# A decoder layer on one core: attention numerator computed transposed, x transposed by DMA, and a new order on every engine

## The reference, cut to what matters

```python
# 1. linear attention with positive features phi (64 per head)
phi = (exp(proj(x) - |x|^2 / (2 sqrt(d))) + 1e-6) / sqrt(m)
kv, ksum = phi_k^T v, sum(phi_k)
out = (phi_q kv) / (phi_q . ksum);   x = layernorm(x + out @ Wo.T + bo)
# 2. softmax attention: queries from x, keys and values from ctx_1024
x = layernorm(x + softmax(q k^T / 4) v)
# 3. gated FFN, 256 -> 1024 -> 256: weights rounded to -1, 0, 1 (scale = mean |w|),
#    activations rounded to 8 bits (scale = row maximum)
x = layernorm(x + bitlinear(silu(bitlinear(x, w_gate)) * bitlinear(x, w_up), w_down))
```

## Time and profile before

| | |
|---|---|
| median of 3 runs | 566.46 us (565.43 to 566.99) |
| the profiled execution, its own time | 565.91 us |
| span of that execution (first to last instruction) | 564.2 us |
| PE busy | 486.1 us (86%) |
| DVE busy | 472.4 us (84%) |
| ACT busy | 411.2 us (73%) |
| POOL busy | 387.6 us (69%) |

### The profile page before, as it was taken

How to read it: one execution, slowest core, us unless ns; L and a number is a source line. 1 busy time by engine, 2 the same in 40 slices (tenths; PEclk the granted TensorE clock), 3 DMA queues, 4 the chain that set the end, 5 groups by cost and what they waited for, 6 DMA issues and landing times.

```text
span 564.2 us, 17426 instructions
## 1 busy us (share of the span) xinstructions
PE 486.1 (86%) x5932; PEld 345.5 (61%) x5990; DVE 472.4 (84%) x1380; ACT 411.2 (73%) x811; POOL 387.6 (69%) x768
## 2 busy tenths in 40 slices
PE   3056999999999998999999999999999998977651
PEld 2034766677667676777777777777777776654320
DVE  0784565889999998999999999999999998998671
ACT  0226667778888887888888888888888887867531
POOL 7032665677777777788777777788788876665432
PEclk9576999999999999999999999999999999998765
DMA  5604776566877775556565656566555587473111
GB/s 142 221 0 82 138 133 110 87 122 122 135 131 133 132 125 110 125 124 131 117 130 120 130 118 130 119 129 124 121 125 123 124 124 122 87 113 67 41 45 37
DMA packets 192649, 64.14 MB, mean 114 GB/s; under 512 B 172384, under 2 KB 192352, under 8 KB 192608
## 3 DMA queue, kind: packets, MB, share of 16 engines
q1 hardware_dynamic: 190080, 60.46, 55.3%
q10 hardware_dynamic: 2528, 3.15, 1.7%
HBM read 17.31 MB, written 4.19 MB: 38 GB/s over the span
## 4 chain that ended last, share of the span: by engine, by line
PE 60%; DVE 12%; DMA 9%; ACT 7%; issue 4%; SPq 4%; POOL 4%; ACTq 0%; POOLq 0%; DVEq 0%
PE bank L1084 9%; PE bank L1151 8%; PE bank L1274 5%; DMA hqT<-hq 5%; PE bank L1244 5%; PE bank L1297 4%; PE bank L1167 3%; PE bank L1104 3%; PE bank L1149 3%; PE bank L1133 2%; PE bank L1099 2%; PE bank L1181 2%; PE bank L1261 2%; DMA tT<-nmT 2%; PE bank L1224 1%
## 5 line engine op out<-in xcount | busy, mean ns | idle before, releaser
L1084 PE MATMUL bank<-wq_hi,xT 128*128 128x512 f16 (+1 forms) x256 | 71.7, 336 | 0.9 <-ACT xT L511 0.7
L1151 PEld LDWEIGHTS bank<-kvm,phq 128*128 128x128 f32 x512 | 62.2, 192 | 2.5
L1151 PE MATMUL bank<-kvm,phq 128*128 128x34 f32 x512 | 59.8, 272 | 0.0
L416 POOL TENSOR_TENSOR pkA<-qk,pkA 128x512 f16<-128x512 f32 x32 | 37.6, 1176 | 31.7 <-ACT pkA L511 31.6
L466 POOL TENSOR_TENSOR xq<-xm,nmagic 128x256 bf16<-128x256 f32 x32 | 19.6, 613 | 51.5 <-DVE xm L911 51.5
L430 POOL TENSOR_TENSOR rs<-ve,mhalf 128x1 f32<-128x1 f32 x96 | 52.9, 552 | 0.0
L865 DVE TENSOR_REDUCE negm<-bank 128x4 f16<-128x512 f32 x64 | 43.8, 685 | 8.6 <-PE bank L1200 8.5
L555 ACT ACTIVATE x<-y,nmr,rs 128x256 f32<-128x256 f32 x64 | 38.3, 599 | 11.1 <-DVE y L976 9.7
L915 DVE SCALAR_TENSOR_TENSOR g<-th,bank 128x512 f32<-128x512 f32 x64 | 43.2, 676 | 3.7 <-ACT th L643 3.6
L1244 PE MATMUL bank<-pT,ctxv 128*32 128x128 f32 x1024 | 42.4, 284 | 4.5 <-ACT pT L620 4.3
L511 ACT ACTIVATE pkT<-bank 128x512 f16<-128x512 f32 x32 | 19.1, 597 | 37.0 <-PE bank L1181 37.0
(11 more groups left out here) (180 smaller groups left out, 1611.5 us busy)
## 6 DMA issues: line engine op xcount, KB each, us to landing
xs<-in_x_dram SPq DMA_DIRECT2D x32, 128.0 KB, 2.5
xr<-in_x_dram SPq DMA_DIRECT2D x32, 128.0 KB, 2.2
cs<-in_ctx_dram SPq DMA_DIRECT2D x32, 128.0 KB, 2.2
out_dram<-ot SPq DMA_DIRECT2D x32, 128.0 KB, 1.9
ffn_ld<-in_L_ffn_w_gate_dram ACTq DMA_DIRECT2D x1, 1024.0 KB, 5.5
ffn_ld<-in_L_ffn_w_up_dram ACTq DMA_DIRECT2D x1, 1024.0 KB, 8.7
ffn_ld<-in_L_ffn_w_down_dram ACTq DMA_DIRECT2D x1, 1024.0 KB, 10.5
pkAT<-pkA SPq DMA_TRANSPOSE x64, 3.2
```

The costliest lines, as they stand in the source:

```text
L1084: last = T.matmul(o, xT[:, 2 * part + c, :], w[:, c, cols], start=(n == 0), stop=(n == 5))
L1151: last = T.matmul(at_num[:, 2 * DV * k:2 * DV * (k + 1)], phq[:, par, k, :], kvm[:, k, :, :].rearrange("p h d -> p (h d)"), start=False, s ...
```

## The change

The numerator is computed transposed. Now the sums are stationary (64 rows, 32 columns) and the features stream past (128 columns): 16 matmuls instead of 8, each on half of the rows and a quarter of the columns of the array, the even heads into one PSUM bank and the odd ones into another. The mask is gone, because each matmul takes only the rows of its own head; `kvm_` is a plain copy on ScalarE. The result lies with heads on partitions, so ScalarE copies it out (`nT_`, two copies) and TensorE transposes it back (`ntp`, four transposes); `rd` and `at` then read that. The 1e-6 of the query features is added on GpSimd (`phe`, 128x1024 in place). For this layout `kvs` puts heads 4j to 4j+3 into column group j; before, groups changed with every head pair.

x is transposed by a transfer of SyncE (`xT_`) instead of `xTp` on TensorE and `xT_` on ScalarE. Five conversions on GpSimd are now `tensor_scalar`. The bn_stats and bn_aggr instructions of the layernorms stand apart in DVE's list.

The weight work is cut into single steps: `once(step, i, n)` puts one step at a place of iteration n. GpSimd makes the identities first; the clearing of large tiles moved to DVE; the biases, Wo and the derived constants are awaited only at the first use (`first_time`). All engines have a new list, and the PSUM tensors lie in other banks.

```diff
             def xT_(t, par):
+                wait_ahead(sp, t, par, ("xlo", 0), ("vm", -2))
+                transpose(xT[:, par, :, :], xpk[:, :, :].rearrange("p n d -> p (n d)"), "xT", par)
...
+            def phe(t, par):
+                wait_ahead(pool, t, par, ("ephq0", 0))
+                g.tensor_scalar(phq[:, par, :, :], phq[:, par, :, :], PHI_EPS, 1.0, ALU.add, ALU.mult).then_inc(
+                    done["phe"], 1)
...
-                g.tensor_tensor(hq[:, 0, :], hm[:, 0, :], nmagic[:, :].to_broadcast([P, 512]),
-                                ALU.add).then_inc(done["hq0"], 1)
+                g.tensor_scalar(hq[:, 0, :], hm[:, 0, :], 1.0, -MAGIC, ALU.mult, ALU.add)
...
+            def kvm_(t, par):
+                wait(act, "kvp", t)
+                sc.activation(kvm[:, :, :, :], at_kv.rearrange("p (k j c) -> p k j c", k=2, j=4),
+                              ACT.Copy).then_inc(done["kvm"], 1)
+
+            def nT_(t, par):
+                wait(act, "nump", t)
+                sc.activation(nT[:, 0:4:2, :], at_num_e.rearrange("p (c t) -> p c t", c=2), ACT.Copy)
+                sc.activation(nT[:, 1:4:2, :], at_num_o.rearrange("p (c t) -> p c t", c=2),
+                              ACT.Copy).then_inc(done["nT"], 1)
...
-            def kvm_(t, par):
-
-                wait(dve, "kvp", t)
-                v.tensor_tensor(kvm[:, :, :, :],
-                                at_kv.rearrange("p (c e) -> p c e", e=32)[:, :, 0:DV].unsqueeze(2).to_broadcast(
-                                    [P, PAIRS, 2, DV]), kvmask[:, :, :, :], ALU.mult).then_inc(done["kvm"], 1)
...
             def kvs(t, par):
...
                 for h in range(H):
-                    j, q = (h // 2) % 4, 2 * (h // 8) + h % 2
+                    j, q = h // 4, h % 4
...
             def nump(t, par):
-
-                wait(pe, "kvm", t)
-                T.matmul(at_num, epsc[:, :], kvm[:, :, :, :].rearrange("p c h d -> p (c h d)"), start=True, stop=False)
-                for k in range(PAIRS):
-                    last = T.matmul(at_num[:, 2 * DV * k:2 * DV * (k + 1)], phq[:, par, k, :],
-                                    kvm[:, k, :, :].rearrange("p h d -> p (h d)"), start=False, stop=(k == PAIRS - 1))
+                wait_ahead(pe, t, par, ("kvm", 0), ("phe", 0))
+                for j in range(4):
+                    for k in range(2):
+                        for odd, o in enumerate((at_num_e, at_num_o)):
+                            rows = slice(64 * odd, 64 * odd + 64)
+                            last = T.matmul(o[32 * j:32 * j + 32, k * P:(k + 1) * P], kvm[rows, k, j, :],
+                                            phq[rows, par, 2 * j + k, :], start=True, stop=True)
                 last.then_inc(done["nump"], 1)
 
+            def ntp(t, par):
+                wait(pe, "nT", t)
+                for q in range(4):
+                    last = T.transpose(at_nt[:, q * P:(q + 1) * P], nT[:, q, :], idf[:, :])
+                last.then_inc(done["ntp"], 1)
...
             def s1(t, par):
+                wait(pe, "m0", t)
                 wait(pe, "ephk1", t, 3)
-                wait(pe, "at", t, 2)
...
+        def once(step, i, at):
+
+            if isinstance(i, int) and i == at:
+                step()
...
-            run(dve, iteration, between={0: (quantise_gate,), 1: (quantise_rest,)})
+                once(scales_of[0], i, 2)
...
+                once(magnitudes[0], i, 1)
+                once(scales_of[2], i, 4)
...
-            run(pe, iteration, between={0: (ffn_means,), 1: (transpose_gate,), 2: (transpose_rest,)})
+                once(ffn_means, i, 2)
```

More of the change, by code:

```diff
@@ L1 @@
 from contextlib import ExitStack
+from functools import partial
 import concourse.bass as bass
@@ L260, in go, with first_time, run @@
                 step(t, (par + lag) % 2)
-        def run(eng, iteration, lags=LAGS, first=FIRST, between={}):
+        def once(step, i, at):
+            if isinstance(i, int) and i == at:
+                step()
+        def first_time(eng, t, tile, semaphore, v):
+            if isinstance(t, int) and t == tile:
+                eng.wait_ge(semaphore, v)
+        def run(eng, iteration, lags=LAGS, first=FIRST):
             for i in range(first):
                 iteration(i, i % 2)
-                for prepare in between.get(i, ()):
-                    prepare()
             with eng.Fori(first, TILES - 1, 2) as i:
@@ L543, in sq @@
+            evacuate = [partial(evacuate_ffn, n) for n in range(6)]
             def sq(t, par):
@@ L631, in oxT_ @@
             def oxT_(t, par):
-                wait(act, "pv1", t)
+                wait(act, "pv0", t)
                 copy(oxT[:, :, :], at_pv.rearrange("p (c t) -> p c t", c=4), "oxT")
@@ L1019, in _ @@
+                go(vsm, i, par, 2)
+            run(dve, iteration)
         @block.tensor
@@ L1079, in project, with transpose_ffn @@
-            def project(o, cols, name):
+                T.matmul(at_means, onesf[:, :], wsum[:, :], start=True, stop=True).then_inc(wmeans, 1)
+            def transpose_ffn(n):
+                pe.wait_ge(ternary, 3 * (n // 2) + 3)
+                dst = at_prep[n].bitcast(BF16)
+                for k in range(8):
+                    if n < 4:
+                        src = ffn_q[:, n // 2, k * D + (n % 2) * P:k * D + (n % 2 + 1) * P]
+                    else:
+                        src = ffn_q[:, 2, (k % 2) * F + (4 * (n - 4) + k // 2) * P:
+                                    (k % 2) * F + (4 * (n - 4) + k // 2 + 1) * P]
+                    last = T.transpose(dst[:, k * P:(k + 1) * P], src, idb[:, :])
+                last.then_inc(ffn_ps, 1)
@@ L1081, in project @@
+            ternaries = [partial(transpose_ffn, n) for n in range(6)]
+            orf_pair = orfp[:, :, :].rearrange("p h m -> p (h m)")
+            def project(o, cols, par, name):
                 n = 0
@@ L1083, in project @@
                     for part, w in ((0, wq_hi), (0, wq_lo), (1, wq_hi)):
-                        last = T.matmul(o, xT[:, 2 * part + c, :], w[:, c, cols], start=(n == 0), stop=(n == 5))
+                        last = T.matmul(o, xT[:, par, 2 * part + c, :], w[:, c, cols], start=(n == 0), stop=(n == 5))
                         n += 1
@@ L1163, in wo @@
             def wo(t, par):
-                wait(pe, "aT", t)
-                wait(pe, "gl1", t, -4)
+                first_time(pe, t, 0, prep, 14)
+                first_time(pe, t, 0, prep_ev, 4)
+                wait(pe, "tlo", t, -1)
                 for k in range(2):
@@ L1229, in st1 @@
             def st1(t, par):
-                wait(pe, "v", t, 5)
+                wait_moved(pe, "row", t, par)
+                wait(pe, "hu0", t, -2)
+                wait(pe, "kvm", t, 3)
                 for k in range(4):
@@ L1249, in pv0 @@
                 wait(pe, "p0", t)
-                wait(pe, "tlo", t, 1)
                 weigh(0, par, "pv0")
@@ L1254, in pv1 @@
                 wait(pe, "p1", t)
-                wait(pe, "pv0", t)
+                wait(pe, "ad3", t, -3)
                 weigh(1, par, "pv1")
@@ L1321, in iteration @@
+                if isinstance(i, int) and i == 5:
+                    pe.wait_ge(done["qk"], 5)
+                once(ternaries[2], i, 5)
                 go(dn, i, par, 9)
-                go(vm, i, par, 1)
-                go(tm, i, par, 5)
-                go(kvp, i, par, 3)
+                go(st1, i, par, 6)
+                go(st0, i, par, 6)
+                go(nump, i, par, 3)
                 go(wo, i, par, 4)
-                go(st0, i, par, 6)
-                go(xTp, i, par, 0)
-                go(st1, i, par, 6)
@@ L1329, in iteration @@
-                go(nump, i, par, 3)
-            run(pe, iteration, between={0: (ffn_means,), 1: (transpose_gate,), 2: (transpose_rest,)})
+                once(ffn_means, i, 2)
+                go(phk1, i, par, 2)
+                if isinstance(i, int) and i == 5:
+                    pe.wait_ge(prep_ev, 4)
+                once(ternaries[3], i, 5)
+                go(ntp, i, par, 3)
+                go(phk0, i, par, 2)
+                go(pv1, i, par, 6)
+                go(pv0, i, par, 6)
+                go(s0, i, par, 5)
@@ L1333 @@
+                go(qkm, i, par, 0)
+                go(xqTp, i, par, 7)
+                go(oxp, i, par, 6)
+                go(phq1, i, par, 2)
+                go(phq0, i, par, 2)
+            run(pe, iteration)
 _INS = ["x", "ctx_1024", "L0_attn_Wq", "L0_attn_bq", "L0_attn_Wk", "L0_attn_bk", "L0_attn_Wv", "L0_attn_bv",
```

722 lines of the change are left out of this document (374 added, 348 removed), and 11 rows, old and new, of the table done.

## The result

The changed kernel takes 524.47 us (median of 4 runs, 523.84 to 525.61), against 566.73 us of the kernel before on the same chip: ratio 0.926, 95% interval 0.9235 to 0.9283. The forecast was 522. The change also raised `FIRST`, the number of iterations written out ahead of the loop, from 14 to 18 (the excerpts of the change leave this out); the last experiment shows that this costs time. The profiled execution took 523.84 us, its span 522.1.

A forecast was written before the change was run, and what follows sets the result against it. TensorE bounds the kernel before; after, DVE was to be the bound at 13.55 us a tile. 102 to the ninth qk + 311.7 + 106 = 519.7 span, plus 1.7 outside, 521.4, said as 522; range 507 to 548, the forecast's own 512 to 530.

The forecast's parts named there:

- the four stages: Span cut at DVE's qk: 21 us to the first, 81 to the ninth, 311.7 for 23 intervals, 106 to the end.
- TensorE's tile: Steady stage, TensorE per tile: 14.57 less 2.70 removed, plus 0.65 numerator and 0.44 transposes back, 12.96 us.
- weaker form: TensorE looks ahead four instructions but not eight, hitting kvs alone: 13.6 to 14.1 us per tile; counted within the first rival.
- strict order: Third rival: column groups do not run side by side in kvs and nump; TensorE 15.2 us per tile, 569 us; chance 0.06.
- the first rival: Steady stage: waits between lists, or GpSimd at its upper price, set a period of 14.1 to 14.3, 537 us; chance 0.19.
- DVE's tile: Steady stage, DVE per tile: 13.75 busy less the masked copy's 0.43, 13.32, plus 0.2 to 0.25 idle, 13.55 us.
- GpSimd: Steady stage, GpSimd per tile: phe 1.2 and conversions 2.4 make 10.8 us, no bound; 13.95 at the dearest.
- SyncE and transfers: Steady stage: SyncE has slack for a sixth transpose per tile; DMA engines some 0.72 busy; x's transpose on no path.
- Start: Up to the first qk: waits for x alone, with a 3.2 us transpose; 21 us (18 to 25) instead of 32.5.
- Fill: First to ninth qk, eight iterations: 76.7 + 9.5 - 5 = 81 us instead of 85.8; ninth qk at 102.
- End: Last qk to the end: three nearly full iterations gain 1 us each, the rest chain-bound; 106 us instead of 107.5.
- The lost start: Second rival: FFN weights delay x, a longer one-tile chain bounds the fill; ninth qk at 112, 531 us; chance 0.10.

The follow-up runs named there:

- the last experiment: 26 iterations written out ahead of the loop instead of 18, against the changed kernel with kvs issued across alternating column groups; 517.74 us, ratio 0.9126 to the kernel before.
- the spread order: Changed kernel with kvs issued so that two heads in succession stand in different column groups; 511.58 us, ratio 0.9000 to the kernel before.
- A later run: On the changed kernel with kvs spread: x loaded first, GpSimd's output-bias wait moved to first use, FFN loads after tile 0's x transpose; 506.51 us, ratio 0.8914.

## Why the prediction was right, and where not

**The time** was 524.5 against 522, and the four stages came within 6 us each. That the sum is closer than its parts is luck: the first qk came 3.9 us late, the 23 intervals took 4.1 more, the end 5.4 less. And two errors hid each other in the steady stage, and the bound that I named was wrong.

**TensorE's tile.** Forecast 12.96; removed and added pieces were right (`nump` 0.64 for 0.65, `ntp` 0.44). The step that failed is the one that left `kvs` at 0.63: it costs 1.36, and TensorE's tile became 13.4. The forecast's "weaker form" of strict order (look-ahead past four instructions, not eight; TensorE at 13.6 to 14.1) was this mechanism, and was put down to the first rival with a small chance. With the regrouping undone TensorE's tile is 0.992 x 12.77 = 12.67, 0.3 less than the 12.96 I summed. Most of that is in where the sum starts: 14.57 is the period before, and TensorE was busy for 98.5% of it, 14.35 us. From there the same pieces give 12.74. The 0.07 left are `kvs` at 0.60 for 0.63 and a rest that no run tells apart.

**DVE's tile.** Forecast 13.55 with idle, and the bound; it is 12.96 busy in the changed kernel and 12.75 with the spread order. The term that I mis-sized is 13.32 busy: I took every remaining instruction as unchanged, and `nlo` lost 0.2 us a tile since GpSimd's conversions read one operand. The other 0.16 are spread over small steps, which no run takes apart. The idle of 0.2 was too much as well: with the spread order DVE has 0.02.

So the sum said max(12.96, 13.55) where the chip had max(13.5, 13.0). The forecast of the steady stage was right for a wrong reason: the two numbers are close, and belong to different engines.

**GpSimd**: `phe` 1.06 for 1.2, conversions 0.47 to 0.65; 83.6% of 13.5 is 11.3 against 10.8. No bound, as said. **ScalarE**: 93.9% of 13.5 is 12.7 for 12.91.

**SyncE and transfers**: said to have slack. In the loop that holds. In the written-out part it doesn't; the 0.23 us by which the mean interval of 13.73 lies above 13.50 arise there.

**Start**: 24.9 for 21, since the transpose took 7.44 and not 3.2 us, and x came 1 us late. A later run shows that the first qk is worth less than it moves: 9.8 us there became 2.3 us at the ninth and some 5 us of the time. **Fill**: 80.9 for 81. **End**: 100.6 for 106; what shortened it by 6.9 us instead of 1.5 was not tried. Nor was it tried which edits brought the ninth qk 12.5 us forward, beyond the sums' part above, and no run undoes the transposed numerator or the new lists alone: what is shown is the pace of the steady stage, not the share of each edit in it.

**Rivals**: of the first, a period of 14.2 from waits or GpSimd, only its "weaker form" happened, at 13.5. Strict order for both steps (569) did not: `nump` runs at 0.64. The lost start (531, with the ninth qk at 112) held in part: 3.9 us late at the first qk, and 3.8 at the ninth, which came at 105.8 for 102.

## What to carry to other kernels

When a change re-indexes which quarter of the array a small matmul uses, write down the run of instructions per place (column group and rows) before and after: four in a row were nearly free here, eight doubled the step, and the engine was the bound. Once two or three engines stand above 94%, test an addition in two places before you name the bound; one that costs its whole length in one place can be free in another. And take the durations of one engine's instructions as constants only if what runs beside them on another keeps its form and its place. A sum for an engine starts from its busy time, not from the period.

## What the runs showed of the hardware that I had not expected

- Eight matmul instructions of 32 stationary columns (all 128 rows) in a row for one column group, 32 in all: 1.36 us; the same 32 in runs of four 0.63, alternating 0.60. Eight in a row for one column group, in pairs on alternate halves of the rows (`nump`, 128 moving columns): 0.64, alternating column groups 0.60.
- A DVE `tensor_tensor` of 128x32 that reads SBUF and starts just after GpSimd's conversion takes 300 ns if that has one operand and 693 ns if it has two; beside the one with two it takes 296 ns where it starts first.
- The DMA transpose of x, which lands in 2.5 us in the steady stage, takes 6.55 to 8.26 us beside loads of weights.
- Eight iterations written out cost 7 us against the same eight in a loop, 0.9 us each, in a kernel whose SyncE has 10.5 us of issuing in a tile of 12.8. The page "Runtime: NRT & Kernel Launch" of the Trainium skill (section Instruction fetch mechanics) calls the fetch of instructions mostly hidden and unrolling the preferred form; the measurement goes against that here.
